# One half of the last weight split moves from GpSimd to VectorE, and the last chunk of the feed-forward is narrowed column half by column half

## The reference

```python
h = relu(layernorm(x))
hs, ht = layer_norm(h, ln1), layer_norm(h_target, ln1)      # the same ln1 scale and bias
q, k, v = ht @ Wq + bq, hs @ Wk + bk, hs @ Wv + bv
probs = softmax(where(adj != 0, q k^T / sqrt(32), -1e30))   # 8 heads, 2048 x 2048
ht = ht + (probs v) @ Wo + bo
y  = layer_norm(ht, ln2)
out = x + (y + gelu(y @ W1) @ W2)                           # W1 256 x 1024, W2 1024 x 256
```

## Time and profile before

| what | value |
|---|---|
| median of 3 runs | 499.89 us (499.8 to 501.54) |
| the profiled execution's own time | 502.69 us |
| its span, first to last instruction | 500.8 us |
| TensorE, share of the span busy | 95% |
| mean granted TensorE clock | 0.987 |

### The profile page before, as it was taken

How to read it: one execution, slowest core, us unless ns; L and a number is a source line. 1 busy time by engine, 2 the same in 40 slices (tenths; PEclk the granted TensorE clock), 3 DMA queues, 4 the chain that set the end, 5 groups by cost and what they waited for, 6 DMA issues and landing times.

```text
span 500.8 us, 10602 instructions
## 1 busy us (share of the span) xinstructions
PE 477.0 (95%) x4364; PEld 245.4 (49%) x4364; DVE 416.5 (83%) x616; ACT 376.4 (75%) x455; POOL 309.9 (62%) x153
## 2 busy tenths in 40 slices
PE   3899979999999999999999999999999799999995
PEld 1466633333433343333433343333345688888884
DVE  5788579999999999999999999998997577565252
ACT  4786978998988998988998998999994370727150
POOL 2000008995998999999999998999999300000000
PEclk9899998999999999999999999999999899999998
DMA  8997689822633674222763300160000100202021
GB/s 254 250 192 115 125 247 403 297 43 44 211 58 55 68 172 80 43 45 48 82 171 66 64 3 3 36 178 2 1 1 3 45 21 23 84 2 84 0 85 45
DMA packets 53231, 46.94 MB, mean 94 GB/s; under 512 B 35454, under 2 KB 46108, under 8 KB 52668
## 3 DMA queue, kind: packets, MB, share of 16 engines
q1 hardware_dynamic: 50672, 37.30, 28.0%
q0 software_dynamic: 2480, 8.92, 10.7%
q10 hardware_dynamic: 28, 0.01, 0.0%
HBM read 31.93 MB, written 14.81 MB: 93 GB/s over the span
## 4 chain that ended last, share of the span: by engine, by line
PE 60%; DVE 16%; issue 13%; POOL 5%; ACT 4%; DMA 1%; DVEq 0%; POOLq 0%
PE acc L1316 13%; PE slot L1301 13%; DVE probs L971 10%; PE acc L1334 6%; PE slot L1416 3%; PE slot L1415 3%; PE slot L1414 3%; PE acc L1429 3%; PE acc L1431 3%; PE acc L1430 3%; PE slot L1214 3%; POOL added_up L527 3%; PE slot L1232 2%; PE slot L1367 2%; DVE stats L812 1%
## 5 line engine op out<-in xcount | busy, mean ns | idle before, releaser
L971 DVE SCALAR_TENSOR_TENSOR probs<-maskT,slot 128x1024 f32<-128x1024 uint16 x256 | 298.3, 1217 | 8.3 <-PE slot L1301 7.8
L713 ACT ACTIVATE probs<-probs 128x1024 f32<-128x1024 f32 x256 | 267.0, 1057 | 25.8 <-DVE probs L971 7.4
L527 POOL TENSOR_TENSOR added_up<-added_up,probs 128x1024 f32<-128x1024 f32 x96 | 226.7, 2401 | 1.2 <-ACT probs L713 1.0
L1316 PE MATMUL acc<-probs,V 128*32 128x512 f32 x1024 | 137.2, 608 | 1.0 <-ACT probs L713 1.0
L1334 PE MATMUL acc<-probs,ones 128*32 128x256 f32 x1024 | 77.1, 379 | 0.0
L1334 PEld LDWEIGHTS acc<-probs,ones 128*32 128x32 f32 x1024 | 33.3, 110 | 72.8 <-issue 71.2
L1301 PE MATMUL slot<-q_hi,k_hi 32*128 32x512 f32 x512 | 64.7, 496 | 3.8 <-DVE probs L971 3.5
L524 POOL TENSOR_TENSOR added_up<-probs 128x1024 f32<-128x1024 f32 x16 | 38.0, 2395 | 31.0 <-ACT probs L713 20.5
L1301 PEld LDWEIGHTS slot<-q_hi,k_hi 32*128 32x128 f32 x512 | 24.6, 182 | 62.1 <-DVE probs L971 55.3
L770 ACT ACTIVATE g_full<-slot 128x512 f32<-128x512 f32 x32 | 19.3, 602 | 46.9 <-issue 30.9
L1301 PE MATMUL slot<-q_lo,k_hi 32*128 32x512 f32 x512 | 52.0, 392 | 0.0
(11 more groups left out here) (130 smaller groups left out, 489.0 us busy)
## 6 DMA issues: line engine op xcount, KB each, us to landing
adj_raw<-in_adj POOLq DMA_DIRECT2D x16, 512.0 KB, 5.8
xs<-in_x SPq DMA_DIRECT2D x4, 512.0 KB, 7.0
htn<-in_L_gnn_h_target SPq DMA_DIRECT2D x4, 512.0 KB, 6.8
ht_saved<-htn SPq DMA_DIRECT2D x1, 2048.0 KB, 7.6
k_hi_saved<-k_hi SPq DMA_DIRECT2D x1, 2048.0 KB, 10.6
k_lo_saved<-k_lo SPq DMA_DIRECT2D x1, 2048.0 KB, 14.1
v_saved<-V SPq DMA_DIRECT2D x1, 2048.0 KB, 9.3
inverse<-inverse_saved SPq DMA_DIRECT2D x8, 256.0 KB
```

The source lines that it names most:

```text
L527: nc.gpsimd.tensor_tensor(added_up[:, pair], added_up[:, pair], at(i), ALU.add).then_inc(added, 1)
L713: nc.scalar.activation(p, p, ACT.Exp).then_inc(exped, 1)
L971: nc.vector.scalar_tensor_tensor(out=probs[:, u % RING], in0=m, scalar=-HALF_EDGE, in1=slot[u % SLOTS][:], op0=ALU.add, op1=ALU.min).then_ ...
L1316: mm = pe.matmul(acc[HD * j:HD * j + HD, 0, :], V[:, i, h * HD:(h + 1) * HD], probs[:, (PAIRS * k + j // 2) % RING, j % 2, :], start=(i == 0),
```

## The change

1. GpSimd no longer makes `w2_lo`; VectorE does, between `y_apply(0)` and `add_residual(2)`, by the same subtraction of 128 x 2048 elements. 2. Both `make_residual(LAST, ...)` of GpSimd now stand behind the wait for `y_lo_out`; the wait for `norm_y` ahead of the first is gone. 3. For the last chunk `narrow_last` runs over the column half d outside and over f inside. Four transposes of the first column half stand in the midst of the second half's matmuls and go to `slot4[0]`. The second half is joined, transposed, finished in two steps. 4. The last chunk's results are stored by three DMAs in place of two: all four tiles of the first 128 columns (512 bytes a row), then two times two tiles of the other 128. `finish_last` takes the place of `join(LAST)` and `finish(LAST)`.

```diff
             sp:
-            for c in range(NCH):
+            def store_last(ts, ds, results):
+                sp.wait_ge(summed, TILES * LAST + results)
+                sp.dma_start(out_rows[:, rows_of(LAST), ds][:, ts, :], result[:, ts, ds]).then_inc(stored, 16)
+
+            for c in range(LAST):
...
-            sp.wait_ge(stored, 32 * NCH)
+            store_last(slice(0, TILES), slice(0, P), TILES)
+            for half in range(2):
+                store_last(slice(half * TILES // 2, (half + 1) * TILES // 2), slice(P, D),
+                           TILES + (half + 1) * TILES // 2)
+            sp.wait_ge(stored, 32 * LAST + 48)
             pool:
-            pool.wait_ge(w2_hi_made, 1)
-            nc.gpsimd.tensor_tensor(w2_lo[:], w2_raw, w2_hi[:].bitcast(F32), ALU.subtract).then_inc(w2_lo_made, 1)
-
-            pool.wait_ge(norm_y, LN2)
+
+            pool.wait_ge(y_lo_out, DC)
             make_residual(LAST, 0)
-            pool.wait_ge(y_lo_out, DC)
             make_residual(LAST, 1)
             dve:
+            def finish_last():
+                def join_part(d, at, width):
+                    ts = slice(at, at + width)
+                    nc.vector.tensor_tensor(out_T[:, d, ts], acc[:, d, ts], yT[LAST % 2][:, d, ts], ALU.add
+                                            ).then_inc(joined, 1)
+
+                def result_part(t, d):
+                    n, ds = LAST * TILES + t, slice(d * P, (d + 1) * P)
+                    nc.vector.scalar_tensor_tensor(out=result[:, t, ds], in0=slot4[0][:, t, ds], scalar=nodes[:, n:n + 1],
+                                                   in1=xr[:, t, ds], op0=ALU.mult, op1=ALU.add).then_inc(summed, 1)
+
+                dve.wait_ge(out_turned, 2 * LAST)
+                dve.wait_ge(narrowed, DC * LAST + 1)
+                join_part(0, 0, CHUNK)
+                dve.wait_ge(x_again, 16 * NCH)
+                dve.wait_ge(stored, 32 * LAST)
+                dve.wait_ge(out_turned, 2 * LAST + 1)
+                for t in range(TILES):
+                    result_part(t, 0)
+                dve.wait_ge(narrowed, DC * NCH)
+                for half in range(2):
+                    join_part(1, half * CHUNK // 2, CHUNK // 2)
+                for half in range(2):
+                    dve.wait_ge(out_turned, 2 * LAST + 2 + half)
+                    for t in range(half * TILES // 2, (half + 1) * TILES // 2):
+                        result_part(t, 1)
+
+            def split_second_weight():
+                dve.wait_ge(w2_hi_made, 1)
+                nc.vector.tensor_tensor(w2_lo[:], w2_raw, w2_hi[:].bitcast(F32), ALU.subtract).then_inc(w2_lo_made, 1)
...
             y_apply(0)
+            split_second_weight()
             add_residual(2)
...
-                join(c)
+                if c < LAST:
+                    join(c)
...
-            finish(LAST)
+            finish_last()
             pe:
+            def narrow_last():
+
+                pe.wait_ge(summed, TILES * LAST)
+                for d in range(DC):
+                    for f in range(FC):
+                        pe.wait_ge(gelu_lo, LAST * FC + f + 1)
+                        ds, dst = slice(d * P, (d + 1) * P), acc[:, d, :]
+                        pe.matmul(dst, w2_hi[:, f, ds], g_hi[:, f, :], start=(f == 0), stop=False)
+                        pe.matmul(dst, w2_hi[:, f, ds], g_lo[:, f, :], start=False, stop=False)
+                        mm = pe.matmul(dst, w2_lo[:, f, ds], g_hi[:, f, :], start=False, stop=(f == FC - 1))
+                        if d == 1 and f == FC // 2:
+                            pe.wait_ge(joined, DC * LAST + 1)
+                            for t in range(TILES):
+                                turned_mm = pe.transpose(slot4[0][:, t, 0:P], out_T[:, 0, t * P:(t + 1) * P], ident[:])
+                            turned_mm.then_inc(out_turned, 1)
+                    mm.then_inc(narrowed, 1)
+                for half in range(2):
+                    pe.wait_ge(joined, DC * LAST + 2 + half)
+                    for t in range(half * TILES // 2, (half + 1) * TILES // 2):
+                        mm = pe.transpose(slot4[0][:, t, P:D], out_T[:, 1, t * P:(t + 1) * P], ident[:])
+                    mm.then_inc(out_turned, 1)
...
-                narrow(c)
+                if c < LAST:
+                    narrow(c)
+                else:
+                    narrow_last()
...
-            turn_out(LAST)
```

More of the change, by code:

```diff
@@ L455, in _ @@
                     sp.dma_start(out_rows[:, rows_of(c), :][:, ts, :], result[:, ts, :]).then_inc(stored, 16)
-                if c < LAST:
-                    sp.dma_start(xr[:], x_rows[:, rows_of(c + 1), :]).then_inc(x_again, 16)
+                sp.dma_start(xr[:], x_rows[:, rows_of(c + 1), :]).then_inc(x_again, 16)
                 if c == LAST - 1:
```

## The result

The changed kernel took 497.8 us in the median of 5 executions (497.29 to 499.66); the kernel before, 501.2 us in the median of 5 (499.8 to 502.9), the three on which the forecast stood among them. The ratio is 0.993, with a 95% interval of 0.9902 to 0.9958: faster by 3.4 us, where 5.45 was forecast, and 497.8 lies above the range, which ended at 497.0. The profiled execution after took 499.66 us with a span of 497.8, against 502.69 and 500.8.

The account below looks back on a forecast made before the run. TensorE was taken as the bound, with a 3.1 us hole before turn_y(0) and slow matmuls behind it. 4.7 + 0.5 + 0.25 = 5.45 us, off the 499.89 us median, gave 494.4 us; range 492.8 to 497.0.

Parts of the forecast that it names:

- The stall of the tensor_scalar by GpSimd, part 1: At y_root(0), before turn_y(0): without GpSimd's w2_lo the tensor_scalar falls from 3.51 to 0.17 us; TensorE gains 3.1 us.
- `w2_lo` on VectorE: Between y_apply and add_residual(2): the subtraction takes 2.3 us on VectorE and costs nothing, hidden by attend(1).
- The residuals, part 3: At the feed-forward's start: GpSimd's later residuals shift VectorE's g_lo by at most 0.7 us; price nothing, 0.6 us of cover.
- The results of the end: Last chunk: the final four results end at about 496.95 instead of 497.46, a gain of 0.5 us.
- The sign for it: At the end: some 1.7 us from the last matmul's release to the last result would show the gain.
- the fall of the clock behind the hole: From turn_y(0) to widen(0): TensorE at full clock once its idle wait is gone, 1.56 us less, taken whole.
- The term of the store: Last store, with half the bytes: 0.25 us less; bounds 0.3 us more or 0.8 us less.
- part 4's 0.75: The last chunk's end: 0.5 us from earlier results and 0.25 us from the last store.
- (c): At y_root(0): the long tensor_scalar was not GpSimd's doing and stays; only the end gains, 499.1 us; chance 0.07.
- (a): Before widen(0): the idle hole goes, but the clock falls anyway or VectorE's w2_lo gates widen; 496.0 us; chance 0.13.
- (b): At g_lo and y_root(1): GpSimd's residuals hold VectorE beyond the 0.6 us of cover, costing 0.7 us; 495.1 us; chance 0.05.
- (d): At the end: the tensor_scalar stall stays and the short-row last store lands in 4.2 us; 500.6 us; chance 0.05.

Follow-up runs that it names:

- the experiment with the early residual: The changed kernel with GpSimd's make_residual(LAST, 0) waiting for norm_y again, beside VectorE's w2_lo; 500.39 us, measured once.
- the kernel before with the filled opening: The kernel before plus five unread matmuls in TensorE's idle stretches at about 15, 70 and 73 us; 499.83 us, ratio 0.9953.
- the lowest group: Three of twelve executions of the kernel before with the filled opening, at 498.15 to 498.31 us.
- the changed kernel with the filled opening: The changed kernel plus the same five unread matmuls in TensorE's idle stretches of the opening; 494.84 us, ratio 0.9851.
- parts 1 to 3 with the filled opening: The changed kernel with the five unread opening matmuls, but the last chunk as in the kernel before; 495.07 us.

## Why the prediction was wrong

**Point by point.** The stall of the tensor_scalar by GpSimd, part 1: right, 3.51 to 0.17 us; TensorE, not VectorE, then sets the start of `turn_y(0)`, as said. `w2_lo` on VectorE: 2.29 us, hidden; TensorE ran through from 379 to the feed-forward. The residuals, part 3: the first `g_lo` was held, took 1.58 us and ended 0.56 behind GpSimd's last instruction at 399.52; that is 0.89 us more than its usual 0.69, where the worst case had 0.7; TensorE has no idle time from 400 to 410, so the cover was enough. The Trainium skill's rule on two SBUF inputs (SBUF — State Buffer, section Who interferes with whom) was not shown by any row of before; the rows after, and the experiment with the early residual, agree with it, with 1.58 against 0.69 us and 4.34 against 2.35. The results of the end, 0.65 for 0.5: right in size. The sign for it, "some 1.7 us from the last matmul's release to the last result", does not agree with the prediction's own working (494.8 to 496.95, or 2.15); 2.09 was measured.

**The step that failed** is the one that turned the sum into a time: "it stood 2.80 above the median of 499.89, and from that the forecast is 494.4 us". In the profiled execution itself the sum was nearly right: 4.98 + 0.65 - 0.43 = 5.2 us for 5.45. But 1.68 of them are the fall of the clock behind the hole. I took it as belonging to the kernel ("I take all of it"), and took it off a median over executions of which only some have it: of four profiled executions with the full hole three have it and one has not, and in the kernel before with the filled opening three of twelve times are those without it. What holds in every execution is 3.3, the stretch from `attend(0)` to `widen(0)` without the fall (19.09 - 15.79), as the lowest group (3.4) shows too. Worse, the median of three, 499.89, was itself low: the median of five was 501.2, and over 81 executions the mean is 501.67, with times from 499.15 to 503.93. So of the 3.4 us between forecast and measurement 1.3 are the base (501.2 for 499.89) and 2.1 the gain (3.4 for 5.45); of these 2.1, part 4 makes up 0.75. The profile had given the hint: 2.80 us between its own time and the median, in one program, had to be something, and I carried it along as a constant.

**The term of the store** was 0.25 us of gain and measured 0.43 of loss in this pair, 0.65 in the mean of seven profiles against seven. That is outside the bound of 0.3 that it was given. I had called half the bytes and a short issue the gain; the issue did fall from 1.10 to 0.38 us, and the landing did not follow. With it all of part 4's 0.75 is gone.

Of the rivals, (c) came nearest in its time (499.1) and (a) next (496.0), both with a wrong mechanism: the long tensor_scalar was gone, the clock did not fall at this place after the change, and VectorE did not gate it. (b) happened on VectorE, and was hidden. (d) did not happen, but its doubt about the short stores was right in direction: they landed in 3.2 to 3.7 us.

What stays open is whether the changed kernel loses more in the opening than the one before. By the traces the mean gain should be 3.4 us plus 1.6 times the share of executions that had the fall: 4.6 if that share is three in four, 4.2 if it is a half. The means differ by 3.7, and with standard deviations of 1.2 and 1.3 us over 24 and 81 executions that is uncertain by 0.6 (two standard errors). So 4.2 is within reach of luck and 4.6 is not. Whether the place of the instructions has a part in it was not tried.

The fastest version here is the changed kernel with the filled opening, 494.84 us, faster than both: 0.9851 of the kernel before. As part 4 is worth nothing, parts 1 to 3 with the filled opening (495.07 us) do as well, with simpler code.

## What to carry to other kernels

Where TensorE has gaps of 1.3 to 1.9 us early in a kernel, a few filler matmuls into a place that will be overwritten can cost nothing and remove both a slow stretch and most of the spread between runs; do this before small changes are measured, for then 0.4 us can be read on one chip where before 1 us could not. Before a small saving is taken off a median, list the stretches of low granted clock in the profiled execution and ask of each whether the other runs have it. A small instruction of VectorE whose length jumps from 0.17 to 3.5 us and ends with a GpSimd instruction is a stall, not work; put work of the two engines that reads two SBUF tiles at different times. Size a term of a few tenths by more than one profile of each kernel.

## What the runs showed of the hardware beyond what I expected

The same instructions up to `attend(0)` took about 375.4, 377.1 or 379.3 us in the unfilled kernels, in the kernel before and in the changed one, by the clock that was granted from 10 to 30 and from 60 to 90 us: 1.00 and 0.94, 0.91 and 0.94, 0.83 and 0.89. That is as much as the whole change was worth. The Trainium skill (TensorE: Matmul & The Clock Gate, Part 1: The HAM clock gate) says of the slow matmuls at a kernel's start that their number varies from run to run of one kernel, and puts their cost at under 1% of a typical span. The stretches here come later, behind idle time at 17 and 72 us, which that sentence does not speak of; they vary from run to run as well, and the 4 us are 0.8% of the span.

Idle time of about 3.1 us came before the fall in three profiled executions and before no fall in one; with 1.74 us it was likewise both ways, and a hole of 0.42 us had none behind it in the one that was looked at.
